# A recommendation tower on one core: all gathers of a tile in one run, and dots that wait for it

## The chip, the core and the metric

The kernel runs on one core of a Trainium2 chip. The core has TensorE (matmuls, called PE in the profile, with PEld for its weight loads), VectorE (DVE), ScalarE (ACT), GpSimd (POOL) and SyncE (SP, which here only issues transfers). Each has its own stream of instructions, and they wait for each other by semaphores. The metric is the device time of one execution in microseconds, and the median over several runs is compared.

## The reference

For each of 2048 samples there are 128 dense features and 26 categorical ids. Each id picks a row of 128 floats from its own table (1000 to 125000 rows). With the dense vector that makes 27 vectors of length 128. All 351 pairwise dot products of them go, with the dense features twice, through a small network:

```python
e = jnp.stack([tbl_0[ids[:, 0]], ..., tbl_25[ids[:, 25]]], axis=1)
combined = jnp.concatenate([dense_features[:, None, :], e], axis=1)
interactions = jnp.einsum('bfd,bgd->bfg', combined, combined)
z = jnp.concatenate([dense_features, interactions[:, _IU0, _IU1]], axis=1)
h = jnp.concatenate([z, r_dense_features], axis=1)
h = jnp.maximum(h @ W_top1 + b_top1, 0.0)
h = jnp.maximum(h @ W_top2 + b_top2, 0.0)
y = h @ W_top3
```

## The kernel before

The batch is cut into 16 tiles of 128 samples, and four tiles make a block. The 26 embedded features of a sample come in two ways.

Sixteen features are *gathered* (`GATHERED`): GpSimd issues one indirect DMA per tile and feature (line 682), which fetches 128 rows of 512 bytes into `rows`. `rows` has places for two tiles (`ROW_TILES = 2`), so the gathers of tile t+2 go where those of tile t were, and may start when TensorE has transposed these. The transposes (`turn_group`, line 806) bring a tile's 16 gathered features into the layout of `combined`, in four groups of four features. VectorE (line 1044) and ScalarE (line 916) copy the groups out of PSUM in turn.

The other ten are *looked up* by matmul, for a block at a time: VectorE makes one-hot columns from ids (line 1031; some on ScalarE), and TensorE multiplies chunks of a whole table with them (line 727), twice, as the table is split in a high and a low part. A feature takes 8 or 10 chunks, in two halves; `half_done` counts the halves. ScalarE copies the result out (line 878) and moves it into `combined` tile by tile (line 897).

When all 27 vectors of a tile stand in `combined`, TensorE makes the dots (`dot_tile`, line 821): 128 small matmuls in four banks. ScalarE copies them out (line 925), SyncE stores them to a scratch in HBM and loads them back in the layout of the network's input, and TensorE computes the network's layers in pieces ("products") between other work (lines 757 to 783).

The order of TensorE's stream is written out: `START` (the ten looks of block 0, with tile 0's transposes put in after `LOOKS_BEFORE_TURN` of them), and then for every tile t the dots of t, the transposes of tile t+1, and the looks and products of `work_after(t)`:

```python
work(START)
for t in range(TILES):
    dot_tile(t)
    work(STEPS[t])
```

So between the transposes of a tile and its dots lie four to six halves of looks and some products. In the last block there are no looks left, only products.

GpSimd issues the gathers of tiles 0 and 1 at the start. Then, for t from 0 to 13, it issues those of tile t+2 in four parts: the first group when tile t has been transposed; the second and third when TensorE has done certain halves of looks (`halves_beside`); the fourth when three of the four banks of tile t's dots are done. Nobody but the transposes of tile t+2 waits for a gather.

Of the kernel before, what the change touches and what calls it, by code (L numbers as in the profile page):

```python
# [13 lines left out]
TILES = BATCH // P  # L14
PER_BLOCK = 4
BLOCKS = TILES // PER_BLOCK
LAST = BLOCKS - 1
# [13 lines left out]
SLOT_FEATURES = [6, 3, 10, 23, 2, 4, 8, 11, 12, 13, 14, 15, 16, 18, 19, 21, 1, 5, 7, 9, 17, 20, 0, 22, 24, 25]  # L31
SLOT_VECTORS = [0] + [f + 1 for f in SLOT_FEATURES]

GATHERED = [16, 16, 16, 16]
MOST_GATHERED = max(GATHERED)
IN_BLOCK = [FEATURES - n for n in GATHERED]
BLOCK_OF = [m for m in range(BLOCKS) for _ in range(IN_BLOCK[m])]
# [4 lines left out]
LOOK_SLOT = [s - FIRST_LOOK[m] if m % 2 == 0 else FIRST_LOOK[m + 1] - 1 - s for s, m in enumerate(BLOCK_OF)]  # L42
# [9 lines left out]
LOOK_PLACES = 15  # L52
SPLIT_AHEAD = 2
# [5 lines left out]
    TABLE_PLACE.append(s if s < TABLE_PLACES else TABLE_PLACE[2 * FIRST_LOOK[m] - 1 - s if AGAIN[s] else s - TABLE_PLACES])  # L59
HIGH, LOW = range(2)  # L60

GROUPS = [[4, 4, 4, 4] for _ in range(BLOCKS)]
IN_QUAD = 4
QUADS = P // IN_QUAD

ROW_TILES = 2
# [7 lines left out]
FILLS = QUADS // PER_BANK  # L74
# [21 lines left out]
HALVES_AFTER = [[6, 5, 5, 4] for _ in range(LAST)]  # L96
# [10 lines left out]

ACT_HOTS = [1, 2, 4, 5, 7, 8]

LOOKS_BEFORE_TURN = 4  # L110

START_IDS_AHEAD = 5

DENSE_AFTER = 1

HIGH_BEFORE_TURN = 6
HIGH_PAIR = 6


def high_after(s):  # L120

    if s == HIGH_BEFORE_TURN - SPLIT_AHEAD or s == HIGH_PAIR + 1:
        return []
    return [s + SPLIT_AHEAD, s + SPLIT_AHEAD + 1] if s == HIGH_PAIR else [s + SPLIT_AHEAD]


def group_slots(t, g):

    sizes = GROUPS[t // PER_BLOCK]
    first = sum(sizes[:g])  # L130
    return range(first, first + sizes[g])


def n_groups(t):
    return len(GROUPS[t // PER_BLOCK])


def groups_by(t):

    return sum(n_groups(i) for i in range(t + 1))  # L140
# [7 lines left out]
def odds_by(t):  # L148

    return sum(n_groups(i) // 2 for i in range(t + 1))  # L150


def turn_use(t, g):
# [29 lines left out]

def look_place(s):

    return BLOCK_OF[s] % 2 * (LOOK_PLACES - IN_BLOCK[0]) + LOOK_SLOT[s]


def chunks_before(s):
# [24 lines left out]

def hots_by_dve(half):
    return half + 1 - hots_by_act(half)


def halves_beside(t, g):

    before = 2 * IN_BLOCK[0] + sum(HALVES_AFTER[i // PER_BLOCK][i % PER_BLOCK] for i in range(t - 1))
    return before + 1 + (g - 1) * HALVES_AFTER[(t - 1) // PER_BLOCK][(t - 1) % PER_BLOCK] // 2


def free_places(half):
# [87 lines left out]
def moves_by(t):  # L313

    return sum(len(move_parts(tile)) for tile in range(t + 1))
# [47 lines left out]
def build(nc, dense, ids, ids_by_feature, tables, W1, b1, W2, b2, W3, y):  # L363
    with ExitStack() as ctx:
# [9 lines left out]
        all_ids = sb("all_ids", [P, TILES, MOST_GATHERED], I32)  # L374
        spread_ids = sb("spread_ids", [P, ID_PLACES, COLS], I32)
        rows = sb("rows", [P, ROW_TILES, MOST_GATHERED, D])
# [71 lines left out]
        gathered = [[sem(f"gathered{i}_{g}") for g in range(max(len(of) for of in GROUPS))] for i in range(ROW_TILES)]  # L448
# [6 lines left out]
        half_done = sem("half_done")  # L455
        look_copied = sem("look_copied")
        look_moved = sem("look_moved")
        turned_done = sem("turned_done")
# [35 lines left out]
        def landed(t, g):  # L494

            return gathered[t % ROW_TILES][g], 16 * gathered_by(t, g)
# [179 lines left out]

        @block.gpsimd
        def _(pool):
            def gather(t, groups):
                for g in groups:  # L680
                    for slot in group_slots(t, g):
                        nc.gpsimd.indirect_dma_start(  # L682
                            rows[:, t % ROW_TILES, slot, :], None, tables[SLOT_FEATURES[slot]][:, :],
                            bass.IndirectOffsetOnAxis(ap=all_ids[:, t, slot:slot + 1], axis=0)).then_inc(gathered[t % ROW_TILES][g], 16)

            nc.gpsimd.memset(ones[:], 1.0).then_inc(ones_ready, 1)
            nc.gpsimd.memset(identity[:], 0.0).then_inc(identity_cleared, 1)
            nc.gpsimd.memset(all_combined[:, P * VECTORS:], 0.0).then_inc(constants_ready, 1)
            for c in chunk_row:
                nc.gpsimd.iota(chunk_row[c][:], pattern=[[1, c]], base=0, channel_multiplier=c,  # L690
                               allow_small_or_imprecise_dtypes=True).then_inc(constants_ready, 1)
            pool.wait_ge(identity_cleared, 1)
            nc.gpsimd.affine_select(out=identity[:], in_=identity[:], compare_op=ALU.not_equal, fill=1.0, base=0,
                                    pattern=[[-1, P]], channel_multiplier=1).then_inc(constants_ready, 1)
            pool.wait_ge(ids_loaded, 16)
            for t in range(ROW_TILES):
                gather(t, range(n_groups(t)))
            for t in range(TILES - ROW_TILES):

                pool.wait_ge(turned_done, groups_by(t))  # L700
                gather(t + ROW_TILES, range(1))
                for g in range(1, n_groups(t + ROW_TILES) - 1):
                    if 0 < t <= LAST * PER_BLOCK:
                        pool.wait_ge(half_done, halves_beside(t, g))
                    gather(t + ROW_TILES, range(g, g + 1))

                pool.wait_ge(dots_done, (t + 1) * FILLS - 1)
                gather(t + ROW_TILES, range(n_groups(t + ROW_TILES) - 1, n_groups(t + ROW_TILES)))

        @block.tensor  # L710
        def _(pe):
# [97 lines left out]
            def dot_tile(t):  # L809

                pe.wait_ge(even_copied, evens_by(t))
                pe.wait_ge(odd_copied, odds_by(t))
                pe.wait_ge(dense_copied, t + 1)
                pe.wait_ge(look_moved, moves_by(t))
                for b in range(FILLS):
                    wait_for_use(fill_use(t, b))
                    for q in range(PER_BANK):
                        for j in range(0, IN_QUAD, AT_ONCE):
                            at = ((b * PER_BANK + q) * IN_QUAD + j) * VECTORS
                            row = j // AT_ONCE * HALF_P  # L820
                            last = nc.tensor.matmul(fill_bank(t, b)[row:row + LOADED, q * SQUARE:(q + 1) * SQUARE],  # L821
                                                    all_combined[:, at:at + LOADED], all_combined[:, at:at + SQUARE],
                                                    start=True, stop=True)
                    last.then_inc(dots_done, 1)
# [18 lines left out]
        def _(act):  # L843
            def high_part(s):
                if s >= LOOKS or AGAIN[s]:
                    return
                i, c = TABLE_PLACE[s], CHUNKS[s]
                if s >= TABLE_PLACES:

                    act.wait_ge(half_done, 2 * (s - TABLE_PLACES + 1))  # L850
                act.wait_ge(table_loaded[i], loads_by(s) * 32)
                nc.scalar.copy(high_table[i][0:ROWS_K, 0:c, :], whole_table[i][0:ROWS_K, 0:c, :]).then_inc(table_high, 1)  # L852
# [18 lines left out]
                last.then_inc(act_hot_ready, 1)  # L871

            def copy_look(s):
                if s >= LOOK_PLACES:

                    act.wait_ge(look_moved, moves_by(BLOCK_OF[s - LOOK_PLACES] * PER_BLOCK + PER_BLOCK - 1))
                act.wait_ge(half_done, 2 * (s + 1))
                nc.scalar.copy(looked_up[:, look_place(s), :], look_bank[s % LOOK_BANKS][:]).then_inc(look_copied, 1)  # L878

# [73 lines left out]
            def copy_ends(ends):  # L953
                for kind, *of in ends:
                    if kind == "turn":
                        t, g = of
                        if g == 0 and t > PER_BLOCK and t % PER_BLOCK == 1:
                            high_inputs(t // PER_BLOCK - 1)
                        if g == 0 and t > 0:
                            move_looks(t, 0, FIRST_MOVES[t // PER_BLOCK])  # L960
                        if g % 2 == 1:
                            copy_group(t, g)
                    elif kind == "look":
                        s, = of
                        copy_look(s)
                        m = BLOCK_OF[s]
                        for ahead in high_after(s):
                            high_part(ahead)
                        if s == FIRST_MOVES[0] - 1:
                            move_looks(0, 0, FIRST_MOVES[0])  # L970
                        if s == FIRST_LOOK[m + 1] - 1:
                            move_looks(m * PER_BLOCK, FIRST_MOVES[m], IN_BLOCK[m])
                        if s + SPLIT_AHEAD in ACT_HOTS[1:]:
                            make_half(2 * (s + SPLIT_AHEAD) + 1)
                    elif of[0] < LAST:
                        copy_out(*of)
# [7 lines left out]
            make_half(2 * ACT_HOTS[0] + 1)  # L984
            start = done_in(START)
            copy_ends(start[:LOOKS_BEFORE_TURN])
            high_part(HIGH_BEFORE_TURN)
            copy_dense(0)
            copy_ends(start[LOOKS_BEFORE_TURN:])
            for t in range(TILES):  # L990
# [166 lines left out]
```

## Time and profile before

| | |
|---|---|
| median of 3 timed runs | 380.81 us (379.55 to 381.22) |
| span of the profiled execution | 496.1 us |
| mean granted TensorE clock | 0.904 |
| TensorE matmul busy | 376.0 us, 76% |
| TensorE weight load busy | 301.4 us, 61% |
| VectorE busy | 244.4 us, 49% |
| ScalarE busy | 195.0 us, 39% |
| GpSimd busy | 254.8 us, 51% |

The profiled execution is one execution that the hardware profiler recorded; of its own time the profile gives the span, from its first to its last instruction, and nothing beyond. It is longer than the timed runs, in which nothing is recorded. Busy time on one engine overlaps with that on others, so the shares don't add up to the span. What counts is the chain of work that ended last, and the idle stretches on the engines in it with what ended them. "Issue" stands for time in which an engine waited for nothing that the profile shows.

### The profile page before, as it was taken

What the parts mean: (1) busy time and instruction counts of PE and PEld (TensorE: products, weight loads), DVE (VectorE), ACT (ScalarE), POOL (GpSimd) and SP (SyncE); (2) the same over time, 40 slices, a digit from 0 to 9 for tenths busy, and PEclk for the clock granted to TensorE, in tenths of its full rate; (3) what the DMA queues carried; (4) which work ended last, traced back from release to release, by engine and by line L of the source; (5) the groups of instructions that cost most, each with busy time, mean ns of one, the idle gap of its engine ahead of it and who ended that gap; (6) DMA issues with size and microseconds to landing.
All of it is one profiled execution on the core that took longest, in us unless ns stands there. A gap on an engine that the chain in (4) does not pass through costs nothing.

```text
span 496.1 us, 8109 instructions
## 1 busy us (share of the span) xinstructions
PE 376.0 (76%) x3360; PEld 301.4 (61%) x3360; DVE 244.4 (49%) x174; ACT 195.0 (39%) x261; POOL 254.8 (51%) x266
## 2 busy tenths in 40 slices
PE   1951777858586665978798796969788696879997
PEld 1630656647474554767586666867676455666787
DVE  4740789674919370765725750956566101112133
ACT  3810986414242521525252532434354334344400
POOL 6774540655737363646666554747466564730000
PEclk9985799989989796989998898989899898789899
DMA  8841763259915153456714533536232621123330
GB/s 210 218 134 41 218 187 85 70 156 275 227 29 161 45 155 103 109 150 153 183 46 128 160 87 104 143 93 193 74 89 63 168 73 27 49 63 100 69 71 5
DMA packets 38479, 58.44 MB, mean 118 GB/s; under 512 B 21665, under 2 KB 22561, under 8 KB 38444
## 3 DMA queue, kind: packets, MB, share of 16 engines
q1 hardware_dynamic: 29304, 40.74, 30.3%
q0 software_dynamic: 8192, 16.79, 13.5%
q8 instruction: 26, 0.43, 0.4%
q10 hardware_dynamic: 948, 0.41, 0.4%
q14 instruction: 9, 0.07, 0.0%
HBM read 47.68 MB, written 10.23 MB: 117 GB/s over the span
## 4 chain that ended last, share of the span: by engine, by line
PE 58%; issue 16%; DVE 11%; another core or an unknown queue 8%; SPq 3%; DMA 2%; ACT 2%; DVEq 0%; ACTq 0%
PE look_bank L727 25%; PE short_bank L821 15%; DVE one_hot L1031 8%; PE out_bank L757 6%; PE out_bank L771 4%; PE short_bank L806 4%; PE out_bank L766 3%; SPq L632 2%; DVE all_combined L1044 1%; DVE low_table L1019 1%; DMA spread_ids<-in_ids_by_feature 1%; PE out_bank L783 1%; SPq L621 1%; DMA last_scratch<-all_dots 1%
## 5 line engine op out<-in xcount | busy, mean ns | idle before, releaser
L682 POOL DMA_INDIRECT rows<-in_tbl,all_ids x256 | 253.9, 992 | 191.9 <-PE short_bank L821 81.9
L1031 DVE TENSOR_TENSOR one_hot<-spread_ids,row_bank 128x2048 fp32r<-128x2048 int32 (+3 forms) x80 | 170.7, 2175 | 27.1 <-PE look_bank L727 10.7
L727 PE MATMUL look_bank<-one_hot,high_table 125*128 125x512 f32 x328 | 140.8, 429 | 20.0 <-issue 16.1
L727 PE MATMUL look_bank<-one_hot,low_table 125*128 125x512 f32 x328 | 132.4, 404 | 0.6 <-issue 0.6
L821 PE MATMUL short_bank<-all_combined 128*59 128x54 f32 x2048 | 88.1, 247 | 53.2 <-issue 51.5
L821 PEld LDWEIGHTS short_bank<-all_combined 128*59 128x59 f32 x2048 | 79.7, 162 | 66.7 <-issue 66.5
L1044 DVE COPY all_combined<-short_bank 128x512 f32<-128x512 f32 x32 | 21.8, 691 | 156.2 <-PE short_bank L806 122.3
L727 PEld LDWEIGHTS look_bank<-one_hot,high_table 125*128 125x128 f32 x328 | 64.5, 197 | 40.5 <-issue 23.6
L727 PEld LDWEIGHTS look_bank<-one_hot,low_table 125*128 125x128 f32 x328 | 64.6, 197 | 16.9 <-issue 4.1
L925 ACT COPY all_dots<-short_bank 128x432 f32<-128x432 f32 x64 | 33.1, 518 | 97.1 <-remote 53.7
L878 ACT COPY looked_up<-look_bank 128x512 f32<-128x512 f32 x40 | 23.4, 586 | 120.8 <-remote 45.3
L806 PE MATMUL short_bank<-identity,rows 128*128 128x128 f32 x256 | 40.0, 290 | 38.7 <-issue 22.5
L806 PEld LDWEIGHTS short_bank<-identity,rows 128*128 128x128 f32 x256 | 28.9, 146 | 47.0 <-issue 27.0
L1019 DVE TENSOR_TENSOR low_table<-whole_table,high_table 125x1024 fp32r<-125x1024 f32 (+1 forms) x28 | 34.8, 1243 | 33.5 <-ACT high_table L852 22.7
L897 ACT COPY all_combined<-looked_up 128x1280 f32<-128x1280 f32 (+2 forms) x20 | 39.7, 1985 | 0.2
L852 ACT CAST high_table<-whole_table 125x1024 fp32r<-125x1024 f32 (+1 forms) x28 | 29.7, 1065 | 7.7 <-DMA whole_table<-in_tbl 7.7
L771 PE MATMUL out_bank<-hidden,w 128*128 128x512 f32 (+2 forms) x96 | 32.4, 470 | 0.0
L938 ACT ACTIVATE hidden<-out_bank,bias 128x512 f32<-128x512 f32 x18 | 15.4, 858 | 33.2 <-PE out_bank L757 18.3
L916 ACT COPY all_combined<-short_bank 128x512 f32<-128x512 f32 x32 | 19.9, 674 | 8.4 <-PE short_bank L806 8.4
L771 PEld LDWEIGHTS out_bank<-hidden,w 128*128 128x128 f32 x96 | 16.8, 199 | 6.3 <-issue 4.3
L1053 DVE TENSOR_SCALAR hidden<-out_bank,bias 128x128 f32<-128x128 f32 (+1 forms) x18 | 7.9, 437 | 22.2 <-PE out_bank L766 17.9
L863 ACT ACTIVATE one_hot<-spread_ids,chunk_row 128x512 fp32r<-128x512 int32 x24 | 15.4, 714 | 0.0
(42 smaller groups left out, 183.5 us busy)
## 6 DMA issues: line engine op xcount, KB each, us to landing
whole_table<-in_tbl SPq DMA_DIRECT2D x26, 448.0 KB
spread_ids<-in_ids_by_feature SPq DMA_DIRECT2D x40, 256.0 KB
block_scratch<-all_dots SPq DMA_DIRECT2D x24, 208.0 KB
rows<-in_tbl,all_ids POOLq DMA_INDIRECT x256
block_scratch<-all_dots SPq DMA_DIRECT2D x24, 104.0 KB
pairs<-block_scratch SPq DMA_DIRECT2D x72, 29.2 KB
whole_table<-in_tbl SPq DMA_DIRECT2D x26, 52.0 KB
whole_table<-in_tbl SPq DMA_DIRECT2D x2, 560.0 KB
```

The lines of the kernel that those rows point to most:

```text
L682: nc.gpsimd.indirect_dma_start(rows[:, t % ROW_TILES, slot, :], None, tables[SLOT_FEATURES[slot]][:, :], bass.IndirectOffsetOnAxis(ap=all_ ...
L727: last = nc.tensor.matmul(look_bank[s % LOOK_BANKS][:], table_parts[part][TABLE_PLACE[s]][0:ROWS_K, c, :], one_hot[0:ROWS_K, (chunks_befor ...
L757: last = nc.tensor.matmul(out, w1_parts[weight][0:rows_k, k, i * P:(i + 1) * P], of_parts[of], start=(k == 0 and weight == of), stop=(k == ...
L771: last = nc.tensor.matmul(out, w2[:, k, o * P:(o + 1) * P], hidden1[:, k, a:b], start=(k == 0), stop=(k == last_k))
L806: last = nc.tensor.transpose(turn_bank(t, g)[:, q * P:(q + 1) * P], rows[:, t % ROW_TILES, slot, :], identity[:])
L821: last = nc.tensor.matmul(fill_bank(t, b)[row:row + LOADED, q * SQUARE:(q + 1) * SQUARE], all_combined[:, at:at + LOADED], all_combined[:, ...
L852: nc.scalar.copy(high_table[i][0:ROWS_K, 0:c, :], whole_table[i][0:ROWS_K, 0:c, :]).then_inc(table_high, 1)
L897: nc.scalar.copy(combined[:, :, 1 + GATHERED[m] + slot:1 + GATHERED[m] + slot + b - a], looked_up[:, place:place + b - a, u * P:(u + 1) * ...
L925: nc.scalar.copy(dots_of(h)[:, :, at:at + PER_BANK], fill_bank(t, b)[:, 0:PER_BANK * SQUARE].rearrange("p (q c) -> p c q", q=PER_BANK)).th ...
L1019: nc.vector.tensor_tensor(low_table[i][0:ROWS_K, 0:c, :], whole_table[i][0:ROWS_K, 0:c, :], high_table[i][0:ROWS_K, 0:c, :], ALU.subtract) ...
L1031: last = nc.vector.tensor_tensor(one_hot[:, place:place + n, :], spread_ids[:, s % ID_PLACES:s % ID_PLACES + 1, :].to_broadcast([P, n, COLS]),
L1044: nc.vector.tensor_copy(to, of).then_inc(even_copied, 1)
```

## The change

GpSimd's gathers of a tile are issued without waits between them. Tiles 0 and 1 are gathered at the start as before. Tile 2 follows behind the transposes of tile 0, tile 3 behind those of tile 1 and so on (`GATHERS_BESIDE`, 13 runs of 16). The waits for halves of looks and for dots are gone. TensorE, ahead of the dots of tiles 1 to 13, now waits until all four groups of tile t+2 have landed. In the opening, tile 0's transposes come after eight looks, no longer after four; the order of ScalarE's casts of tables follows (`high_after` goes), and VectorE makes 18 halves of one-hot columns ahead of the first group copies, where it made 10. The places of looked-up columns are computed in a form that also holds for other numbers of gathered features; with 16 in every block they are the same.

```diff
-LOOKS_BEFORE_TURN = 4
+LOOKS_BEFORE_TURN = 8
...
-HIGH_BEFORE_TURN = 6
-HIGH_PAIR = 6
-
-
-def high_after(s):
-
-    if s == HIGH_BEFORE_TURN - SPLIT_AHEAD or s == HIGH_PAIR + 1:
-        return []
-    return [s + SPLIT_AHEAD, s + SPLIT_AHEAD + 1] if s == HIGH_PAIR else [s + SPLIT_AHEAD]
+GATHERS_BESIDE = [16] * 13 + [0]
+TILES_AT_START, TILES_BEFORE_DOTS = 2, 3
...
+def gathers_beside(w):
+
+    rest = [(t, slot) for t in range(TILES_BEFORE_DOTS, TILES) for slot in range(GATHERED[t // PER_BLOCK])]
+    first = sum(GATHERS_BESIDE[:w])
+    return rest[first:first + GATHERS_BESIDE[w]]
...
-            for t in range(ROW_TILES):
-                gather(t, range(n_groups(t)))
-            for t in range(TILES - ROW_TILES):
-
-                pool.wait_ge(turned_done, groups_by(t))
-                gather(t + ROW_TILES, range(1))
-                for g in range(1, n_groups(t + ROW_TILES) - 1):
-                    if 0 < t <= LAST * PER_BLOCK:
-                        pool.wait_ge(half_done, halves_beside(t, g))
-                    gather(t + ROW_TILES, range(g, g + 1))
-
-                pool.wait_ge(dots_done, (t + 1) * FILLS - 1)
-                gather(t + ROW_TILES, range(n_groups(t + ROW_TILES) - 1, n_groups(t + ROW_TILES)))
+            for t in range(TILES_AT_START):
+                gather_tile(t)
+
+            pool.wait_ge(turned_done, groups_by(0))
+            for t in range(TILES_AT_START, TILES_BEFORE_DOTS):
+                gather_tile(t)
+            for w in range(len(GATHERS_BESIDE)):
+
+                pool.wait_ge(turned_done, groups_by(w + 1))
+                for t, slot in gathers_beside(w):
+                    gather(t, slot)
...
                 pe.wait_ge(look_moved, moves_by(t))
+                if 0 < t <= TILES - TILES_BEFORE_DOTS:
+
+                    for g in range(n_groups(t + ROW_TILES)):
+                        pe.wait_ge(*landed(t + ROW_TILES, g))
                 for b in range(FILLS):
...
-                        for ahead in high_after(s):
-                            high_part(ahead)
+                        high_part(s + SPLIT_AHEAD)
...
-            high_part(HIGH_BEFORE_TURN)
```

On GpSimd, in the stream of the kernel before, the gathers of tile 3 stand in four parts (each row is one indirect DMA; `in_tbl_6` is the table of feature 6; the semaphore that an instruction waits for stands in brackets; the rows between the ends of a part are left out):

```order
L682 DMA rows<-in_tbl_6,all_ids 128x128 [waits turned_done]
...
L682 DMA rows<-in_tbl_2,all_ids 128x128 [waits half_done]
...
L682 DMA rows<-in_tbl_12,all_ids 128x128 [waits half_done]
...
L682 DMA rows<-in_tbl_16,all_ids 128x128 [waits dots_done]
...
L682 DMA rows<-in_tbl_21,all_ids 128x128
L682 DMA rows<-in_tbl_6,all_ids 128x128 [waits turned_done]
```

In the changed kernel the same gathers stand at the same place of GpSimd's stream:

```order
L685 DMA rows<-in_tbl_6,all_ids 128x128 [waits turned_done]
...
L685 DMA rows<-in_tbl_2,all_ids 128x128
...
L685 DMA rows<-in_tbl_12,all_ids 128x128
...
L685 DMA rows<-in_tbl_16,all_ids 128x128
...
L685 DMA rows<-in_tbl_21,all_ids 128x128
L685 DMA rows<-in_tbl_6,all_ids 128x128 [waits turned_done]
```

The gathers keep their order; the waits for halves and for dots between them are gone, and the next tile's first gather waits for transposes as before.

On TensorE, in the kernel before, this stands where the looks behind tile 1's transposes end and the dots of tile 1 begin:

```order
L727 MATMUL look_bank0<-one_hot,high_table3 128x512
L727 MATMUL look_bank0<-one_hot,low_table3 128x512
L821 MATMUL short_bank0<-all_combined 59x54 [waits look_moved,dense_copied,odd_copied,even_copied]
L821 MATMUL short_bank0<-all_combined 59x54 x15
L821 MATMUL short_bank1<-all_combined 59x54 [waits even_copied]
```

In the changed kernel, at the same place of TensorE's stream (`gathered1_0` to `gathered1_3` are the semaphores of the four groups of the place that tiles 1 and 3 share):

```order
L733 MATMUL look_bank0<-one_hot,high_table3 128x512
L733 MATMUL look_bank0<-one_hot,low_table3 128x512
L831 MATMUL short_bank0<-all_combined 59x54 [waits gathered1_1,gathered1_0,gathered1_2,look_moved,gathered1_3,dense_copied,odd_copied,even_copied]
L831 MATMUL short_bank0<-all_combined 59x54 x15
L831 MATMUL short_bank1<-all_combined 59x54 [waits even_copied]
```

The order of matmuls is the same; the first dot of the tile also waits for tile 3's four groups of gathers.

## Rows read from the trace of the kernel before

**Rows 1.** The answer on cores, span and mean granted clock.

```profile
core 0: 496.1 us, clock 0.904
```

**Rows 2.** The page: chain; groups (count, busy us, mean ns, idle before, releasers).

```profile
PE 58%; issue 16%; DVE 11%; another core or an unknown queue 8%; SPq 3%; DMA 2%; ACT 2%; DVEq 0%; ACTq 0%
...
L682 POOL DMA_INDIRECT rows<-in_tbl,all_ids x256 | 253.9, 992 | 191.9 <-PE short_bank L821 81.9
...
L821 PE MATMUL short_bank<-all_combined 128*59 128x54 f32 x2048 | 88.1, 247 | 53.2 <-issue 51.5
```

**Rows 3.** TensorE in order of time (start us, us, idle before), tiles 0, 4.

```profile
84.79 3.68 PE L821 MATMUL short_bank<-all_combined 128*59 128x54 f32 x128 [1.42 <-ACT all_combined L897]
...
182.07 1.23 PE L821 MATMUL short_bank<-all_combined 128*59 128x54 f32 x37 [1.47 <-issue]
...
186.05 0.35 PE L821 MATMUL short_bank<-all_combined 128*59 128x54 f32 x2 [1.99 <-issue]
...
192.81 3.79 PE L821 MATMUL short_bank<-all_combined 128*59 128x54 f32 x82 [0.37 <-issue]
```

**Rows 4.** GpSimd in order of time, the same columns, at three places.

```profile
94.00 0.94 POOL L682 DMA_INDIRECT rows<-in_tbl,all_ids  x1 [1.44 <-PE short_bank L806]
...
188.86 0.94 POOL L682 DMA_INDIRECT rows<-in_tbl,all_ids  x1 [0.30 <-issue]
...
202.64 1.24 POOL L682 DMA_INDIRECT rows<-in_tbl,all_ids  x1 [2.04 <-PE short_bank L806]
```

**Rows 5.** Windows, 13 dot stages: stretch, us, PE busy, PEclk, DMA share, GB/s.

```profile
433.90:442.60 8.70, 5.53 (x130) 0.80 0.10 25
sum 126.60, PE 77.15; mean PE 5.93
```

**Rows 6.** Windows, from transposes to dots, tiles 1 and 13, all 13.

```profile
92.90:103.70 10.80, 10.80 (x48) 1.00 0.61 169
...
420.40:433.90 13.50, 10.39 (x37) 0.75 0.17 45
sum 170.20, PE 163.91; mean PE 12.61
```

**Rows 7.** Windows, transposes after dots, 12 stages: the last two and sum.

```profile
384.80:391.80 7.00, 2.77 (x17) 0.89 0.69 179
414.40:420.40 6.00, 3.85 (x32) 1.00 0.18 44
sum 52.90, PE 31.25; mean PE 2.60
```

**Rows 8.** Opening: transposes (window); look 8, VectorE (in order of time).

```profile
33.50:53.00 19.50, 4.50 (x18) 0.63 0.28 77
...
72.79 0.39 PE L727 MATMUL look_bank<-one_hot,low_table 125*128 125x512 f32 x1
...
49.98 1.22 DVE L1019 TENSOR_TENSOR low_table<-whole_table,high_table 125x1024 fp32r<-125x1024 f32 x1 [17.56 <-ACT high_table L852]
```

**Rows 9.** TensorE after idling: one instruction; two windows with the granted clock.

```profile
28.13 0.48 PE L727 MATMUL look_bank<-one_hot,high_table 125*128 125x512 f32 x1 [3.46 <-issue]
...
28.10:31.40 3.30, 3.27 (x9) 0.55 0.84 246
...
192.80:196.60 3.80, 3.79 (x83) 0.62 0.18 70
```

**Rows 10.** DMA queues and issues: packets, MB, share; xcount, KB, us to landing.

```profile
q8 instruction: 26, 0.43, 0.4%
...
last_scratch<-all_dots SPq DMA_DIRECT2D x10, 104.0 KB, 1.9
...
last_scratch<-all_dots ACTq DMA_DIRECT2D x2, 104.0 KB, 2.4
...
out_y<-y_sb SPq DMA_DIRECT2D x1, 8.0 KB, 1.4
```

**Rows 11.** Waits on GpSimd: us in total, times, longest us.

```profile
POOL rows L682 <- issue: 68.3, 224, 0.3
```

More of the change, by code:

```diff
@@ L60 @@
 HIGH, LOW = range(2)
-GROUPS = [[4, 4, 4, 4] for _ in range(BLOCKS)]
+GROUPS = [[4] * (n // 4) + [n % 4] * (n % 4 > 0) for n in GATHERED]
 IN_QUAD = 4
@@ L108 @@
 ACT_HOTS = [1, 2, 4, 5, 7, 8]
-LOOKS_BEFORE_TURN = 4
+LOOKS_BEFORE_TURN = 8
 START_IDS_AHEAD = 5
 DENSE_AFTER = 1
-HIGH_BEFORE_TURN = 6
-HIGH_PAIR = 6
-def high_after(s):
-    if s == HIGH_BEFORE_TURN - SPLIT_AHEAD or s == HIGH_PAIR + 1:
-        return []
-    return [s + SPLIT_AHEAD, s + SPLIT_AHEAD + 1] if s == HIGH_PAIR else [s + SPLIT_AHEAD]
+GATHERS_BESIDE = [16] * 13 + [0]
+TILES_AT_START, TILES_BEFORE_DOTS = 2, 3
+assert sum(GATHERS_BESIDE) == sum(GATHERED[t // PER_BLOCK] for t in range(TILES_BEFORE_DOTS, TILES))
+def gathers_beside(w):
+    rest = [(t, slot) for t in range(TILES_BEFORE_DOTS, TILES) for slot in range(GATHERED[t // PER_BLOCK])]
+    first = sum(GATHERS_BESIDE[:w])
+    return rest[first:first + GATHERS_BESIDE[w]]
 def group_slots(t, g):
@@ L150, in odds_by, with group_of @@
     return sum(n_groups(i) // 2 for i in range(t + 1))
+def group_of(t, slot):
+    return next(g for g in range(n_groups(t)) if slot in group_slots(t, g))
 def turn_use(t, g):
@@ L184, in look_place, with block_before @@
 def look_place(s):
-    return BLOCK_OF[s] % 2 * (LOOK_PLACES - IN_BLOCK[0]) + LOOK_SLOT[s]
+    return BLOCK_OF[s] % 2 * (LOOK_PLACES - IN_BLOCK[BLOCK_OF[s]]) + LOOK_SLOT[s]
+def block_before(s):
+    earlier = [BLOCK_OF[i] for i in range(s) if look_place(i) == look_place(s)]
+    return earlier[-1] if earlier else None
 def chunks_before(s):
@@ L216, in hots_by_dve @@
     return half + 1 - hots_by_act(half)
-def halves_beside(t, g):
-    before = 2 * IN_BLOCK[0] + sum(HALVES_AFTER[i // PER_BLOCK][i % PER_BLOCK] for i in range(t - 1))
-    return before + 1 + (g - 1) * HALVES_AFTER[(t - 1) // PER_BLOCK][(t - 1) % PER_BLOCK] // 2
 def free_places(half):
@@ L678, in _, with gather, gather_tile @@
         def _(pool):
[L679 to L684, printed above, removed]
+            def gather(t, slot):
+                nc.gpsimd.indirect_dma_start(
+                    rows[:, t % ROW_TILES, slot, :], None, tables[SLOT_FEATURES[slot]][:, :],
+                    bass.IndirectOffsetOnAxis(ap=all_ids[:, t, slot:slot + 1], axis=0)).then_inc(
+                        gathered[t % ROW_TILES][group_of(t, slot)], 16)
+            def gather_tile(t):
+                for slot in range(GATHERED[t // PER_BLOCK]):
+                    gather(t, slot)
             nc.gpsimd.memset(ones[:], 1.0).then_inc(ones_ready, 1)
@@ L695, in _ @@
             pool.wait_ge(ids_loaded, 16)
-            for t in range(ROW_TILES):
-                gather(t, range(n_groups(t)))
-            for t in range(TILES - ROW_TILES):
-                pool.wait_ge(turned_done, groups_by(t))
-                gather(t + ROW_TILES, range(1))
-                for g in range(1, n_groups(t + ROW_TILES) - 1):
-                    if 0 < t <= LAST * PER_BLOCK:
-                        pool.wait_ge(half_done, halves_beside(t, g))
-                    gather(t + ROW_TILES, range(g, g + 1))
-                pool.wait_ge(dots_done, (t + 1) * FILLS - 1)
-                gather(t + ROW_TILES, range(n_groups(t + ROW_TILES) - 1, n_groups(t + ROW_TILES)))
+            for t in range(TILES_AT_START):
[6 more added lines that the diff above has]
+                for t, slot in gathers_beside(w):
+                    gather(t, slot)
         @block.tensor
@@ L873, in copy_look @@
             def copy_look(s):
-                if s >= LOOK_PLACES:
-                    act.wait_ge(look_moved, moves_by(BLOCK_OF[s - LOOK_PLACES] * PER_BLOCK + PER_BLOCK - 1))
+                if block_before(s) is not None:
+                    act.wait_ge(look_moved, moves_by(block_before(s) * PER_BLOCK + PER_BLOCK - 1))
                 act.wait_ge(half_done, 2 * (s + 1))
```

## The prediction

> **What bounds the kernel now.** I read the span first, then the chain of waits, then the groups by line, and then, as the chain named TensorE, its work in order of time, stage by stage. The span is 496.1 us [rows 1], and the median of the timed runs is 380.8 us. This gap of 115 us must be understood before any sum is made, as the sum is made against the profiled execution.
>
> The chain gives TensorE 58% and "issue" 16% [rows 2]. Issue is time in which the engine waited for nothing that the profile shows. The groups show where it lies: 51.5 us of it stand before the dots of line 821. In order of time one sees when. The 128 dots of tile 0, with no gather beside them, take 3.68 us; those of tile 4 run 37 matmuls at full pace, then let one or two through at a time for 9 us, and then the last 82 [rows 3]. The gathers ran until 189.8 us in that stretch [rows 4]. The 13 dot stages of tiles 1 to 13 take 126.6 us [rows 5], where 13 x 3.68 = 47.8 would do: 78.8 us of starving. The first tile's transposes, beside the opening gathers, take 19.5 us [rows 8] where later ones take 4: 15.5 us more. Together 94.3 us.
>
> Without them the profiled execution would be 496.1 - 94.3 = 401.8 us. The timed median is 380.8, less still. So in timed executions most, probably all, of this starving is absent. It comes with the recording: the stages that issue TensorE work densest starve, after a first 30 or so matmuls at full pace, and only while gathers are written. I therefore take 401.8 us as the profile's picture of a timed run, and 380.8 / 401.8 = 0.948 as the scale between the two.
>
> Built up forward, the same 401.8 is: dots of tile 0 at 84.8 - 15.5 = 69.3; they and tile 1's transposes 3.7 + 4.4 (until 92.9); then 13 stages of looks and products, 170.2 [rows 6]; 13 of dots, 47.8; 12 of transposes, 52.9 [rows 7]; and 53.5 after tile 13's dots (496.1 - 442.6 [rows 5]). TensorE is in one unbroken loop of about 13.1 + 3.7 + 4.4 = 21.2 us a tile, and bounds the kernel. GpSimd is the second: 16 gathers at 0.944 us with 0.30 between them [rows 4], one per 1.245 us, are 19.9 us a tile, hidden only because they may run beside everything and are not needed until two tiles later.
>
> **The change part by part.** *The gathers in one run.* For tile t+2 the run starts behind the transposes of tile t: 1.1 us after them (92.9 to 94.0 [rows 4]), then 15 x 1.245 + 0.944 = 19.6 us until the last is issued. That it has landed costs more. No row shows a gather's landing; the nearest are stores and loads that land 1.4 to 2.4 us after issue [rows 10]. Nothing at all is the other end, if landing were within the 0.944. I take 2.0, the middle of what lands.
>
> The rows give 0.944 us for a gather and 2.0 for a transfer of another queue. The Trainium skill, "Perfetto Trace Analysis", section "DMA Instruction — SWDGE (GPSIMD)", says that such an instruction's reported window ends when its descriptors are written, and not when data has moved. By this the 2.0 us are to be added; were it not so, the sum below would be 544.1 - 13 x 2.0 = 518.1, and the time 491.
>
> *The dots' wait.* TensorE reaches the dots of tile t on average 13.1 us after its transposes [rows 6], and waits for 1.1 + 19.6 + 2.0 = 22.7. So it stands 9.6 us in each of 13 tiles. What is behind it on its engine are the dots themselves, and behind them the next transposes, which alone release GpSimd's next run. Nothing overlaps across tiles any more: the loop closes through GpSimd, landing, dots and transposes.
>
> *The clock.* After 3.5 us of idling, TensorE's granted clock was 0.55 for the next 3.3 us, and after the starving of tile 4 it was 0.62 over 3.8 us in which 82 dots took 3.79 us [rows 9], against 2.36 at the pace of 128 in 3.68. That is the lower level, 1.2 GHz against 2.4, for about 3.3 us. In a before that doesn't starve this does not arise in these stages; in the changed kernel every dot stage follows a wait of 9.6 us. 3.3 us at half pace do 1.65 us of work, so 1.65 us are added: dots 5.35 us. Ends: nothing, and 3.7.
>
> *The transposes* keep 4.0 us: 52.9 / 12 = 4.4 [rows 7], less what the last two, of 7.0 and 6.0 us, waited for work that the longer loop will have done (5 us over 12 stages). The loop is 1.1 + 19.6 + 2.0 + 5.35 + 4.0 = 32.05 us.
>
> *The opening.* Tile 0's transposes move from behind look 4 to behind look 8. Look 8 ends at 73.2 us [rows 8]; less the 19.5 us of the stage that stood ahead, 53.7, and VectorE, which lost 17.6 us to the same stall [rows 8], allows 54. Transposes done at 58, first gather at 59.1, then tiles 2 and 3 in one go, as tile 1's transposes are done (about 78) before tile 2's run is: 31 x 1.245 + 0.944 = 39.5, and 2.0: dots of tile 1 at 100.6. In the profiled before they start at 103.7; unstarved at 69.3 + 3.7 + 4.4 + 10.8 = 88.2.
>
> *The rest* costs nothing: the order of ScalarE's casts and of the first dense copy moves within an opening that VectorE sets, and ScalarE is 39% busy; the places for looked-up columns and the groups come out the same with 16 gathered throughout. Fewer waits on GpSimd remove instructions that aren't on the path. If ScalarE's cover is gone it is one cast, about 1 us, once.
>
> *The sum.* Dots of tile 1 at 100.6; 12 loops of 32.05, 384.6; tile 13's dots 5.35; the end as before, 53.5. Together 544.1 us, my forecast for the profiled span: 48 us longer than 496.1, as the starving that vanishes (94.3) pays for most of the waits (142.3). A timed run has no starving to give back: 544.1 x 0.948 = 516 us. Adding the difference instead, 380.8 + 142.3, gives 523.
>
> *Bounds.* The unknowns are the pause of 0.30 us between gathers (seen 224 times [rows 11], so I take it, though recording could be in it), landing and clock. With no pause the run is 15.1 us and the loop 27.5: 59.1 + 30.2 + 2.0 = 91.3 for tile 1, + 330 + 5.35 + 53.5 = 480, x 0.948 = 455. At the mean gather, 0.992 with 0.305 between [rows 2, 11], run 20.4 and tile 1 at 102.3: 102.3 + 12 x 32.85 + 58.85 = 555.4; with landing 2.4 and 0.7 us more until the run starts (201.0 to 202.6 in one tile [rows 4]) 13 x 1.1 more, 569.7, x 0.948 = 540.
>
> **The rivals.**
> - *The clock doesn't fall.* For it: 0.55 and 0.62 are two places only. 544.1 - 13 x 1.65 = 522.6, x 0.948 = 495 us. Chance 17%.
> - *No pause between gathers in a timed run.* For it: the timed run is shorter by 21 us than I can explain. Against: the pause is the same to 10 ns beside idle and busy engines. 455 us. Chance 14%.
> - *The starving is in timed runs too.* Then it is given back there: 380.8 - 94.3 + 142.3 = 429 us. Against: an unstarved kernel would take 286 us, while the profile's TensorE loop alone makes 402. Chance 9%.
> - *Faster*, one mechanism: gathers starve TensorE in timed runs as in the profile, and the run is short enough that the dots' wait costs less than the starving did. The price is linear in the interval between gathers: at 1.245 us the waits cost 142.3, at 0.944 they cost 480 - 401.8 = 78. They equal the 94.3 at 0.944 + 0.30 x 16 / 64 = 1.02 us; below that it is faster, at 0.944 by 16 us: 365 us. For it: the before starves exactly where the change keeps gathers away, in 13 stages and one of the opening. Against: it needs two doubtful things at once. Chance 4%.
> - *The dots' waits are met on arrival*, so no change, 381 us. It needs a run of under 11 us, 0.6 us a gather, below the shortest gather written. 2%.
>
> The profile's rows release one or two starved matmuls at a time. The Trainium skill, "Runtime: NRT & Kernel Launch", section "Instruction fetch mechanics", says that an engine's program is streamed in 16 KiB blocks of 256 instructions, by a DMA queue of its own. Starving by this rule would be in timed runs too, and the time 429 us. The trace agrees on the size (26 packets, 0.43 MB [rows 10]), but a late block would stop TensorE between blocks, not after each matmul, so I leave that rival at 9%.
>
> **How the numbers follow.** Forecast 516 us with 52%; the rivals above have 17, 14, 9, 4 and 2%, and 2% lie above 540. The range 455 to 540 holds the forecast, the unfallen clock and the missing pause, 83%. A measurement of this kernel can tell about 0.5% from no change. Faster by more than that 4%, within it 2%, slower 94%.
>
> **What would show it.** In the changed kernel's profile: a span near 544 us; 13 waits of TensorE before the first dot, each some 9 to 10 us, ended by the gathers; 128 dots in about 5.3 us with no issue gaps; granted clock near 0.5 at their start; GpSimd idle only from the landing to the next transposes, 13 us a tile; distance from one tile's dots to the next's 32 us. Starving of the dots after the run has landed, or a loop under 28 us, would make it wrong, as would a timed run that is faster than the profile by much more than 5%.

## The result and the profile after

The changed kernel takes 528.5 us (527.6 to 531.8), the kernel before 380.2 (378.8 to 381.2, four runs now): a ratio of 1.390, with a 95% interval of 1.385 to 1.396. It is slower by 148 us, in the forecast range and 12 us above the forecast of 516. The profiled execution took 528.3 us, with a span of 526.4, at a mean granted clock of 0.851 [rows 1: 496.1 and 0.904].

This is the page of the changed kernel, the chain by engine and the two groups that answer to [rows 2]:

```profile
POOL 40%; PE 22%; issue 15%; DMA 10%; SPq 6%; ACT 4%; DVE 1%; ACTq 1%
...
L685 POOL DMA_INDIRECT rows<-in_tbl,all_ids x256 | 259.7, 1014 | 205.6 <-PE short_bank L812 130.2
L831 PE MATMUL short_bank<-all_combined 128*59 128x54 f32 x2048 | 85.4, 266 | 144.1 <-DMA rows<-in_tbl,all_ids 141.9
```

The chain has turned over: GpSimd's gathers make 40% of it, TensorE 22%. The idle time ahead of the dots is now ended by gathers, and what ends GpSimd's are the transposes. The waits of the changed kernel (us in total, times, longest) show both halves of the loop, with 13 waits each, as the change has it:

```profile
PE short_bank L831 <- DMA rows<-in_tbl,all_ids: 141.9, 13, 15.8
POOL rows L685 <- PE short_bank L812: 130.2, 13, 12.5
POOL rows L685 <- issue: 73.7, 242, 0.3
```

TensorE in order of time, at tile 1, which answers to [rows 3]:

```profile
95.03 6.11 PE L831 MATMUL short_bank<-all_combined 128*59 128x54 f32 x128 [15.83 <-DMA rows<-in_tbl,all_ids]
101.07 2.10 PE L812 MATMUL short_bank<-identity,rows 128*128 128x128 f32 x16
```

Windows over the 13 dot stages (stretch, us, PE busy, PEclk, DMA share, GB/s), which answer to [rows 5, 9]:

```profile
95.00:101.10 6.10, 6.07 (x129) 0.56 0.01 3
...
435.80:442.10 6.30, 6.30 (x129) 0.53 0.01 3
...
sum 73.90, PE 73.73; mean PE 5.67
```

TensorE stood 15.83 us, and the 128 dots then took 6.11, without a gap. The 13 stages have 73.7 us busy where 13 x 3.68 = 47.8 would do, at granted clocks of 0.53 to 0.73. The 16 transposes behind them take 2.10 us, not the 4 of the kernel before's first trace.

GpSimd in order of time, at the end of one run and the start of the next:

```profile
123.13 0.94 POOL L685 DMA_INDIRECT rows<-in_tbl,all_ids  x1 [0.30 <-issue]
134.20 0.94 POOL L685 DMA_INDIRECT rows<-in_tbl,all_ids  x1 [10.13 <-PE short_bank L812]
```

The last gather of the run for tile 4 ends at 124.07, the dots start at 125.82, the transposes end at 133.93, and the next run starts 0.27 us later. Over the 12 loops (dots of tile 1 at 95.03, of tile 13 at 468.65) a loop is 31.13 us: 0.3 until the run starts, 20.7 the run, 2.0 from the last gather's window to the dots (landing), 5.7 dots, 2.1 transposes, and 0.3 on average for the network's third layer, which stands between dots and transposes in two tiles.

### The profile page after: what moved, and what is told of

Same layout as the page of the kernel before. It is cut to its first block, busy times and chain, and to the rows that moved or that the text cites. A ratio compares the mean times of both kernels' runs of the same rounds, so it can differ in the third digit from the quotient of the medians.

```text
span 526.4 us, 8136 instructions
## 1 busy us (share of the span) xinstructions
PE 358.2 (68%) x3360; PEld 297.9 (57%) x3360; DVE 244.2 (46%) x174; ACT 194.2 (37%) x261; POOL 260.7 (50%) x266
## 4 chain that ended last, share of the span: by engine, by line
POOL 40%; PE 22%; issue 15%; DMA 10%; SPq 6%; ACT 4%; DVE 1%; ACTq 1%
POOL rows L685 40%; PE short_bank L831 14%; DMA rows<-in_tbl,all_ids 7%; PE short_bank L812 5%; SPq L637 3%; ACT one_hot L873 2%; SPq L626 2%; DMA whole_table<-in_tbl 2%; DMA last_scratch<-all_dots 1%; PE look_bank L733 1%; ACT high_table L862 1%; ACTq L1019 1%; PE out_bank L789 1%; ACT one_hot L880 1%; DVE one_hot L1039 1%
## 5 line engine op out<-in xcount | busy, mean ns | idle before, releaser
L685 POOL DMA_INDIRECT rows<-in_tbl,all_ids x256 | 259.7, 1014 | 205.6 <-PE short_bank L812 130.2
L831 PE MATMUL short_bank<-all_combined 128*59 128x54 f32 x2048 | 85.4, 266 | 144.1 <-DMA rows<-in_tbl,all_ids 141.9
L831 PEld LDWEIGHTS short_bank<-all_combined 128*59 128x59 f32 x2048 | 83.7, 184 | 151.5 <-issue 151.5
L733 PE MATMUL look_bank<-one_hot,high_table 125*128 125x512 f32 x328 | 136.8, 417 | 16.1 <-DVE low_table L1027 12.7
L733 PE MATMUL look_bank<-one_hot,low_table 125*128 125x512 f32 x328 | 129.3, 394 | 0.0
L733 PEld LDWEIGHTS look_bank<-one_hot,high_table 125*128 125x128 f32 x328 | 62.4, 190 | 36.1 <-DVE low_table L1027 10.6
L733 PEld LDWEIGHTS look_bank<-one_hot,low_table 125*128 125x128 f32 x328 | 62.5, 191 | 15.2 <-issue 2.9
L1027 DVE TENSOR_TENSOR low_table<-whole_table,high_table 125x1024 fp32r<-125x1024 f32 (+1 forms) x28 | 34.7, 1239 | 10.8 <-ACT high_table L862 10.8
L812 PE MATMUL short_bank<-identity,rows 128*128 128x128 f32 x256 | 33.6, 279 | 0.7 <-DVE all_combined L1052 0.7
L777 PE MATMUL out_bank<-hidden,w 128*128 128x512 f32 (+2 forms) x96 | 30.7, 451 | 0.0
L812 PEld LDWEIGHTS short_bank<-identity,rows 128*128 128x128 f32 x256 | 27.7, 141 | 4.1 <-DVE all_combined L1052 1.0
L926 ACT COPY all_combined<-short_bank 128x512 f32<-128x512 f32 x32 | 19.6, 676 | 1.8 <-PE short_bank L812 1.8
```

The lines of the kernel that those rows point to most:

```text
L685: nc.gpsimd.indirect_dma_start(rows[:, t % ROW_TILES, slot, :], None, tables[SLOT_FEATURES[slot]][:, :], bass.IndirectOffsetOnAxis(ap=all_ ...
L733: last = nc.tensor.matmul(look_bank[s % LOOK_BANKS][:], table_parts[part][TABLE_PLACE[s]][0:ROWS_K, c, :], one_hot[0:ROWS_K, (chunks_befor ...
L777: last = nc.tensor.matmul(out, w2[:, k, o * P:(o + 1) * P], hidden1[:, k, a:b], start=(k == 0), stop=(k == last_k))
L812: last = nc.tensor.transpose(turn_bank(t, g)[:, q * P:(q + 1) * P], rows[:, t % ROW_TILES, slot, :], identity[:])
L1027: nc.vector.tensor_tensor(low_table[i][0:ROWS_K, 0:c, :], whole_table[i][0:ROWS_K, 0:c, :], high_table[i][0:ROWS_K, 0:c, :], ALU.subtract) ...
```

## The experiments

**The kernel before, once more.** The first four experiments had spans within 3 us of their own times, and hardly any starving. So the kernel before was recorded again:

> The kernel before once more, unchanged, for its trace. The traces of the first experiments show almost no starving of TensorE, and spans 2 to 3 us under their own times, while the first trace of the kernel before had 496 us against 380. Theory (the starving was in that one recorded execution, not in the kernel): span 377 to 381 us, dots of 3.7 to 5 us, transposes of 2 to 5 us. Rival (the pacing of the gathers in four parts is what makes a recorded execution starve): a span of 490 us again.

One execution: 377.3 us, with a span of 375.4. The timed executions beside the experiments bear it out: 29 of the kernel before are on record with their spans, and these are 375.5 to 382.5 us, 1.8 to 3.2 under their own times. So timed executions leave a record too, and the 496.1 us stand alone. The page of the second trace, chain by engine and GpSimd's group:

```profile
PE 50%; POOL 12%; ACT 10%; SPq 10%; issue 7%; DMA 7%; DVE 4%; ACTq 0%; DVEq 0%
...
L682 POOL DMA_INDIRECT rows<-in_tbl,all_ids x256 | 260.1, 1016 | 79.3 <-issue 77.4
```

The groups by line, dots and transposes of TensorE (count, busy us, mean ns, idle before, releasers):

```profile
L821 PE MATMUL short_bank<-all_combined 128*59 128x54 f32 x2048 | 59.9, 218 | 5.8 <-ACT all_combined L897 2.9 <-issue 2.0 <-ACT all_dots L925 0.8
...
L806 PE MATMUL short_bank<-identity,rows 128*128 128x128 f32 x256 | 36.4, 290 | 7.7 <-DVE all_combined L1044 6.6 <-ACT all_dots L925 0.5 <-issue 0.4
```

TensorE in order of time, at the dots of tile 4, where the first trace had starved for 9 us [rows 3]:

```profile
132.24 3.68 PE L821 MATMUL short_bank<-all_combined 128*59 128x54 f32 x128 [1.48 <-ACT all_combined L897]
135.85 2.10 PE L806 MATMUL short_bank<-identity,rows 128*128 128x128 f32 x16
```

GpSimd in the same stretch:

```profile
132.99 0.95 POOL L682 DMA_INDIRECT rows<-in_tbl,all_ids  x1 [0.30 <-issue]
134.25 0.94 POOL L682 DMA_INDIRECT rows<-in_tbl,all_ids  x1 [0.30 <-issue]
```

The dots take 3.68 us with a gather starting every 1.25 us beside them, and so do ten of the 13 stages; the other three take 4.5 to 5.1, and all 13 together 51.1, where the first trace had 126.6. "Issue" ahead of the dots is 2.0 us in place of 51.5. So the starving belonged to that one recorded execution and not to the kernel. And GpSimd, which the first trace shows idle for 192 us, hardly idles: what it has is the pause of 0.3 us, 254 times, and its 256 gathers run back to back from 3.1 to 340.9 us. TensorE's matmuls are busy for 90% of this span. So both engines are occupied nearly throughout; whether both bound the kernel before, the runs with other gathers have to show.

**The wait taken away, all else of the change kept.**

```diff
-                if 0 < t <= TILES - TILES_BEFORE_DOTS:
-
-                    for g in range(n_groups(t + ROW_TILES)):
-                        pe.wait_ge(*landed(t + ROW_TILES, g))
```

> The changed kernel without the dots' wait for the landed gathers: the run of 16 and the opening stay. Theory (the wait alone makes the time; the starving of TensorE belongs to the profile): timed 375 to 385 us, the same as before, while the profiled span is again far longer, about 480 to 500 us, with dots of 8 to 14 us beside gathers. Rival (one run of 16 without the pacing costs by itself): timed 400 us or more. Rival (starving is in timed runs too): the timed time moves with the stretch of dots beside gathers, here more than in the kernel before, 390 to 400 us.

Measured 385.8 us (385.0 to 388.7), 1.0145 of before (1.0099 to 1.0191), span 385.9. That is a microsecond outside what the theory gave, and short of both rivals; but the profiled span that I expected, 480 to 500, was wrong, which set off the experiment above. The dots' wait is worth 528.5 - 385.8 = 142.7 us, 96% of the change.

**The opening alone**, on the kernel before:

```diff
-LOOKS_BEFORE_TURN = 4
+LOOKS_BEFORE_TURN = 8
...
-                        for ahead in high_after(s):
-                            high_part(ahead)
+                        high_part(s + SPLIT_AHEAD)
...
-            high_part(HIGH_BEFORE_TURN)
```

> The kernel before with the opening alone changed: tile 0's transposes behind eight looks, ScalarE's casts in their plain order. Theory: the profiled span loses the 15 us that these transposes starved (496 to about 481 us), and the timed time stays within 3 us of 380. Rival (starving in timed runs): 365 us.

Measured 384.5 us, 1.0134 of before (1.0079 to 1.0189): slower by 3 to 7 us, 4.6 by the medians. The span is 380.1. That is a miss for both, in the time and in the span. GpSimd in order of time, behind the gathers of tiles 0 and 1, shows what changed:

```profile
46.55 0.94 POOL L682 DMA_INDIRECT rows<-in_tbl,all_ids  x1 [0.30 <-issue]
52.70 0.95 POOL L682 DMA_INDIRECT rows<-in_tbl,all_ids  x1 [5.21 <-PE short_bank L806]
```

It waited 5.2 us for the transposes that now come later; from there on its gathers run back to back to 346.5 us, 5.6 later than in the kernel before, and GpSimd has 45% of the chain, where the second trace of the kernel before gives it 12%. This is the likely cause of the loss, but not the only one: TensorE's own opening is longer as well, as tile 1's dots start at 79.1 us, 2.6 later than in that trace. The two weren't told apart. The run in one piece adds 385.8 - 384.5 = 1.3 us, which the two intervals don't tell from nothing.

**The same opening question asked of the changed kernel**, with 8 set back to 4:

```diff
-LOOKS_BEFORE_TURN = 8
+LOOKS_BEFORE_TURN = 4
```

> The changed kernel with tile 0's transposes behind four looks, as before the change. Theory (GpSimd's stream sets the time from the opening on): it idles 5 us in the opening with eight looks, and tile 2's gathers can follow the first 32 without a pause: 5 to 6 us less, 523 us. Rival (the opening is set by VectorE and the looks): no change. Rival (transposes beside the opening gathers starve, 15 us): more than 530 us.

Measured 522.6 us (520.2 to 526.5), 5.9 us less: the size that the theory gave, but its reason holds only in part. GpSimd did run without the idling of 5 us, and its last gather ahead of tile 1's dots ends 4.6 us sooner (88.68, in the changed kernel 93.24). It took 3.9 us to land, though, and not 1.8, so these dots start 2.5 us sooner (92.55 against 95.03). Of the 8.1 us between the two spans (518.3 and 526.4), 5.1 lie in the 12 loops behind, 4.0 of them in dots (64.9 us against 68.8) that follow much the same waits. Sixteen transposes beside the opening gathers took 2.65 us, not 19.5 [rows 8].

**Three groups waited for, not four.**

```diff
-                    for g in range(n_groups(t + ROW_TILES)):
+                    for g in range(n_groups(t + ROW_TILES) - 1):
```

> The changed kernel, but the dots wait for three of the four groups of gathers (12 of 16), all else the same. Theory (the loop closes through GpSimd's run, at 0.944 us and a pause of 0.30 in timed runs as well): 13 waits shorter by 4 x 1.245 = 5.0 us, 65 us in all: 464 us. Rival (no pause in timed runs): 13 x 3.8 = 49 us less, 479 us. Rival (the wait isn't the bound): under 20 us less.

Measured 459.3 us (457.5 to 462.7), 69.2 less. The waits fell from 141.9 to this:

```profile
PE short_bank L831 <- DMA rows<-in_tbl,all_ids: 80.4, 13, 14.5
```

A loop of this trace is 25.84 us (dots of tile 1 at 93.68, of tile 13 at 403.76), 5.3 shorter than 31.13. Four gathers with the pause of 0.30 behind each are 5.0 us at the median of 0.944 and 5.26 at the mean of 1.014; without the pause they would be 3.8 to 4.1. So the pause is in the loop, and in timed runs too, as the two recorded executions are themselves among the timed ones (528.3 and 462.7 us). This experiment can't tell median from mean; the run of the changed kernel can: 15 x 1.314 + 1.014 is the 20.7 us that it takes, 15 x 1.245 + 0.944 would be 19.6. Tile 1's dots start only 1.4 us sooner than in the changed kernel: the twelfth gather's window ended at 88.2, and they waited until 93.7, with the DMA engines 0.74 busy.

**The clock.** Matmuls of no use keep TensorE at work until the gathers land:

```diff
+                if 0 < t <= TILES - TILES_BEFORE_DOTS:
+
+                    wait_for_use(fill_use(t, 0))
+                    for _ in range(14 if t < 5 else 9):
+                        nc.tensor.matmul(fill_bank(t, 0)[:, 0:512], identity[:], all_combined[:, 0:512],
+                                         start=True, stop=True)
```

The first try had 28 and 18 of them:

> The changed kernel with 18 (tiles 1 to 4: 28) matmuls of identity by 512 columns into the first dot bank, overwritten later, put between TensorE's arrival and its wait for the gathers, so that it isn't idle long there. Theory (the lower clock after the wait makes 128 dots take 5.7 us instead of 3.7): dots back at 3.7 to 4 us, granted clock near 1.0 in them, 13 x 2.0 = 26 us less: about 503 us. Rival (dots are slower beside landing transfers or for another reason): dots stay at 5.7 us and the time at 528 us.

Measured 595.4 us. One of these matmuls takes 0.86 us, so 18 take 15.6 and reach 5 to 7 us past the landing, and 28 reach 8 to 11: the total says nothing. But all 13 dot stages were back at 3.68 us at a granted clock of 1.00. With half as many:

> As the experiment with identity matmuls ahead of the wait, with half as many of them (9, in tiles 1 to 4 14), since one took 0.86 us and 18 reached past the wait. 9 take 7.8 us, 14 take 12.1, under each wait of the changed kernel. Theory (clock): dots at 3.7 us at a granted clock of 1.0, 13 x 2.0 = 26 us under 528.5: about 503 us, a little more where the filler reaches past the wait. Rival: no gain, 528 us, as the loop closes through GpSimd and not through the dots.

Measured 505.0 us (504.1 to 507.5), 23.5 less. Windows over three of its dot stages (PE busy, PEclk, DMA share, GB/s):

```profile
95.20:100.30 5.10, 5.07 (x129) 0.69 0.01 3
125.00:128.70 3.70, 3.70 (x129) 1.00 0.02 4
272.50:276.20 3.70, 3.70 (x129) 1.00 0.25 64
```

In tile 1 TensorE still stood 3.9 us between the filler and the landing, and its dots took 5.1 us at 0.69; so did two others (5.2 us), after waits of 3.5 and 2.1. In the other ten, after waits up to 2.7 us, the dots took 3.68. The dots of the 13 stages fell from 73.7 us to 52.4. So the lower clock behind the wait is worth at least 21 us of the 142.7, 23.5 by the times, with three stages still slow; and TensorE's rate matters here though TensorE is idle a third of the time, as its dots lie in the closed loop.

**Half of the gathers**, in the changed kernel:

```diff
+                    if slot < 8:
+                        gather(t, slot)
-                    gather(t, slot)
```

> The changed kernel with 8 gathers a tile from tile 2 on (the other 8 features keep the rows of tiles 0 and 1, so the output is another). The run is then 8 x 1.3 = 10.5 us and lands about when TensorE arrives. Theory (TensorE's own loop of 13.1 + 3.7 + 2.1 us is what is left): 12 loops of about 19.2 us, 355 to 372 us, a little under the kernel before, whose gathers bind it. Rival (starving by gathers beside dots is real in timed runs and was worth 94 us): 300 us or less. Rival (the wait costs even where it is met): 400 us.

Measured 393.8 us, span 391.4: above the expected range, as there was still a wait in six tiles, 22.5 us in all. In tile 2 the last gather was issued by 100.5 us, and the dots started at 108.4. The window of that stretch has DMA queues 0.81 busy (columns: PE, PEld, DVE, ACT, POOL busy, PEclk, DMA share, GB/s):

```profile
99.50:108.40 8.90, 1.09 (x5) 0.56 (x3) 7.24 (x5) 0.65 (x1) 0.94 (x1) 0.80 0.81 173
```

The landing was late indeed: packets of the gathers' queue run until 107.4 us. SyncE had issued seven loads of tables and ids between 94.2 and 99.4 us, and I take the landing after 8 us, not 2, to be due to such loads; this was not tried by itself. From tile 7 on the waits are under 0.3 us, the dots run at 3.68 us, as most of them do beside gathers in the kernel before. Take off the 22.5 us, four slow dot stages (6.6) and some 5 for the opening, and about 357 us of TensorE's own are left, an estimate.

**Fourteen gathers in the kernel before.**

```diff
-                    for slot in group_slots(t, g):
+                    for slot in group_slots(t, g)[:4 if t < ROW_TILES or g < 3 else 2]:
```

> The kernel before with 14 gathers a tile in place of 16 from tile 2 on (two features keep the rows of tiles 0 and 1, so the output is another), nothing else changed. Its second trace shows GpSimd's gathers back to back from 3 to 341 us. Theory (GpSimd co-bounds the kernel before): 28 gathers of 1.32 us fewer on it, 37 us, of which TensorE's own loop leaves part: 360 to 372 us. Rival (TensorE alone bounds it, as the prediction had it): 377 us or more.

Measured 372.1 us, 0.979 (0.976 to 0.983). So fewer gathers make the kernel before faster, by 7.8 us, at the upper end of what the theory gave, and TensorE alone doesn't bound it. Of the 37 us that GpSimd had less to do, most went into waits for TensorE (22 us in the trace), its last gather ended 20 us sooner, and it is no longer in the chain. The 28 gathers also moved data; that their traffic and not GpSimd's time cost the 7.8 us was not tried. Looking these two features up, in place of gathering them, would cost TensorE 16 matmuls a look, at 48 in 10.8 us [rows 6] 3.6 us, and 22 us for two features in three blocks, an estimate, against 7.8 gained. That was not tried; of the versions run here, none that computes everything beats the kernel before.

## Why the prediction was right, and where it was not

The direction and the mechanism hold: dots that wait for the run's landing close a loop through GpSimd, landing, dots and transposes; 13 waits; a lower clock behind each; nothing in exchange. The size came out within 2.4%, and that is in part luck, as two errors cancelled.

1. *The base was misread.* I took the 94.3 us of starving out of the first trace and kept 401.8 us as the picture of a timed run, with a scale of 0.948 for the rest. The second trace of the same kernel has 375.4, and spans lie 2 us under their times (1.004 in the changed kernel). What I had left in was more starving. The transposes of tiles 1 to 13 were 57.3 us (4.4 + 52.9) and are 36.4, single stages 2.1 to 5.7 us; the first page had shown it:

```profile
L806 PE MATMUL short_bank<-identity,rows 128*128 128x128 f32 x256 | 40.0, 290 | 38.7 <-issue 22.5
```

And the opening had lost 24.8 us, not 15.5: tile 0's dots start at 60.0 us, and at 84.8 in the first trace. The step that failed is the scale: it stood for an unexplained 21 us and should have been a reason to doubt the trace, not a factor. The difference, 380.8 + 142.3 = 523, comes nearer, since an error common to both sums drops out of it; the spans differ by 526.4 - 375.4 = 151.0.

2. *The profiled span* was forecast at 544.1 and is 526.4. Opening: dots of tile 1 at 95.0, forecast 100.6, as GpSimd's first gather of tile 2 starts at 52.7 and not at 59.1. Loops: 31.13, forecast 32.05, of which transposes -1.9 and the start of the run -0.8, against run +1.1 (20.7, as gathers average 1.014 us and not 0.944), dots +0.3 and the third layer +0.3. Landing, 2.0, was right. The end: 52.4, forecast 53.5. Added up, 5.6 + 11.0 + 1.1 = 17.7 us too much; then the scale took 28 off, where the changed kernel's time is 2 above its span.
3. *What bounds the kernel before* was wrong: not TensorE alone with GpSimd hidden. In the second trace the gathers are back to back, and 28 fewer make it 7.8 us faster. The changed kernel's sum isn't hurt by this, as it follows GpSimd from its first wait on; but it has no term for what the later transposes cost by themselves, 4.6 us in the kernel before.
4. *The clock* was right in kind, 1.65 us a tile forecast, 2.0 found, and worth 23.5 us where it was removed in ten of 13 stages.
5. *The rivals.* The missing pause is ruled out by the changed kernel's trace, which is of a timed execution, and by the three-group experiment; the unfallen clock by the windows and the filler. Starving in timed runs is ruled out by the spans of the 29 timed executions, the second trace and the half gathers. With it falls the way in which the change could have gained: the dots of tiles 1 to 13 take 51.1 us beside gathers and would take 47.8 at 3.68, so keeping gathers away from them could save 3.3 us at most. The block fetch of instructions I had weighed by the Trainium skill, "Runtime: NRT & Kernel Launch", "Instruction fetch mechanics". Its 26 packets took 0.9 to 1.5 us each in the first trace as in the second, and only one of them falls into the 9 us that the dots of tile 4 starved (at 185.0): this speaks against it. That a gather's reported window leaves out its landing, as the Trainium skill, "Perfetto Trace Analysis", "DMA Instruction — SWDGE (GPSIMD)", has it, the changed trace bears out: the packets of the gathers' queue go on for 1.2 to 2.4 us behind the last window's end, and 1.75 us and more pass until the dots.

What made the one execution starve stays open. It was recorded once, and none of the ten traces that followed shows it, so nothing could be varied; that the recording did it, as the prediction says, is not shown.

## What to carry to other kernels

Hold a profile's span against the timed median before reading anything in it; where they differ by more than a few microseconds, record the kernel again, since everything in such a trace that looks like contention may belong to that one execution. The span that each timed run leaves, where there is one, settles it sooner. A wait on a producer's newest work turns two engines that run side by side into one loop that adds them up: price it as the whole round (run, landing, consumer, release), with the producer's mean interval and the consumer's clock after idling. And an engine that is only 70% busy by its instructions can be the bound, if a fixed pause follows each of them.

## What the runs showed of the hardware

- GpSimd's indirect gathers of 128 rows of 512 bytes: windows of 0.944 us median and 1.014 mean in the changed kernel (0.99 to 1.04 in the other traces, the longest 2.5), with 0.30 us between two in a row; about 1.32 us each. Beside them 128 dots took 3.68 us in ten of 13 stages of the kernel before's second trace, as without them, and 4.5 to 5.1 in three.
- Landing of the last gather: the dots start 1.75 to 3.0 us after its window's end in the changed kernel, but 8.0 us after it (half gathers, tile 2) and 5.5 us (three groups, tile 1) where the DMA engines were 0.81 and 0.74 busy.
- TensorE's granted clock was 0.53 to 0.73 over the dots behind waits of 8 to 16 us. It also fell behind waits of 2.6 to 14.5 us in the three-group run (0.54 to 0.71), of 2.9 to 7.9 with half the gathers (0.60 to 0.69), and of 2.1, 3.5 and 3.9 in the filler's run, but there not behind others of 2.1 and 2.7, and with half the gathers not behind 1.1 and 1.9.
